# Causal attention with a layer norm and experts: GpSimd's sums of probabilities in four pieces, and the PV matmuls of two key tiles in one run

## What is computed

```python
q = (x @ Wq + bq).reshape(b, s, NQ, D)         # NQ = 16, D = 64
k = (x @ Wk + bk).reshape(b, s, NKV, D)        # NKV = 4
v = (x @ Wv + bv).reshape(b, s, NKV, D)
q = _rotary(q)
k = _rotary(k)
logits = einsum('bqhgd,bkhd->bhgqk', q.reshape(b, s, NKV, g, D), k) / sqrt(D)
logits = where(causal, logits, -1e30)
w = softmax(logits, axis=-1)
out = einsum('bhgqk,bkhd->bqhgd', w, v).reshape(b, s, NQ * D) @ Wo + bo
```

## Time and profile before

| what | value |
|---|---|
| median of 3 runs | 1393.81 us (1393.8 to 1394.24) |
| the profiled execution, its own time | 1390.9 us |
| its span in the profile | 1389.0 us |
| mean granted TensorE clock | 0.972 of 2.4 GHz |
| busy: PE, PEld, DVE, ACT, POOL | 1294.5, 812.5, 919.5, 567.2, 532.4 us |

### The profile page before, as it was taken

How to read it: one execution, slowest core, us unless ns; L and a number is a source line. 1 busy time by engine, 2 the same in 40 slices (tenths; PEclk the granted TensorE clock), 3 DMA queues, 4 the chain that set the end, 5 groups by cost and what they waited for, 6 DMA issues and landing times.

```text
span 1389.0 us, 18379 instructions
## 1 busy us (share of the span) xinstructions
PE 1294.5 (93%) x6732; PEld 812.5 (58%) x6732; DVE 919.5 (66%) x1775; ACT 567.2 (41%) x1178; POOL 532.4 (38%) x503
## 2 busy tenths in 40 slices
PE   3699999988999998999999979999996799999998
PEld 2445555445555554555555545555544688888887
DVE  3767877768687776878777687777747544444443
ACT  1444544544544454454444544453443222232222
POOL 2553346454454554336446345434513211010110
PEclk9699999999999999999999999999997799999999
DMA  5000000000000000000000000000001000000001
GB/s 133 1 0 1 1 1 1 1 1 0 1 0 1 1 1 0 1 1 1 1 0 1 1 1 0 1 1 1 1 1 46 0 24 23 23 23 22 24 1 31
DMA packets 18444, 12.93 MB, mean 9 GB/s; under 512 B 7104, under 2 KB 15680, under 8 KB 18368
## 3 DMA queue, kind: packets, MB, share of 16 engines
q1 hardware_dynamic: 11072, 9.58, 2.3%
q10 hardware_dynamic: 7296, 2.36, 0.7%
HBM read 10.88 MB, written 1.05 MB: 9 GB/s over the span
## 4 chain that ended last, share of the span: by engine, by line
PE 77%; DVE 14%; issue 3%; POOL 3%; ACT 1%; ACTq 1%; DVEq 0%; POOLq 0%
PE PS L1002 17%; PE PS L1050 12%; PE PS L956 10%; PE PS L984 10%; PE PS L1064 8%; PE PS L986 8%; DVE part_max L742 2%; PE PS L1021 2%; PE PS L1012 2%; PE PS L969 2%; DVE k_split L731 2%; DVE full L758 2%; PE PS L933 2%; DVE full L787 2%; PE PS L940 2%
## 5 line engine op out<-in xcount | busy, mean ns | idle before, releaser
L742 DVE TENSOR_REDUCE part_max<-PS 128x1 f32<-128x512 f32 (+2 forms) x576 | 348.8, 620 | 130.0 <-PE PS L956 104.1
L579 ACT ACTIVATE full<-PS 128x512 f32<-128x512 f32 x384 | 224.3, 598 | 230.8 <-PE PS L986 214.6
L956 PE MATMUL PS<-KT,QT 128*128 128x512 f32 (+3 forms) x640 | 263.5, 425 | 9.5 <-ACT QMT L561 5.0
L984 PE MATMUL PS<-QT,KT 128*128 128x512 f32 (+3 forms) x640 | 266.6, 417 | 1.1 <-ACT diag L588 1.1
L986 PE MATMUL PS<-QMT,KT 128*128 128x512 f32 (+3 forms) x640 | 234.4, 366 | 0.0
L448 POOL TENSOR_TENSOR full<-full 128x2048 f32<-128x2048 f32 x32 | 145.7, 4575 | 214.1 <-PE PS L1002 213.6
L956 PEld LDWEIGHTS PS<-KT,QT 128*128 128x128 f32 x640 | 121.7, 193 | 155.8 <-DVE part_max L742 78.8
L1002 PE MATMUL PS<-full,V 128*64 128x512 f32 x768 | 209.5, 624 | 0.0
L588 ACT ACTIVATE diag<-PS 128x512 f32<-128x512 f32 (+3 forms) x256 | 111.3, 438 | 227.9 <-PE PS L989 202.6
L852 DVE TENSOR_TENSOR full<-full,PS 128x512 f32<-128x512 f32 x128 | 88.0, 688 | 145.0 <-ACT full L628 144.9
L984 PEld LDWEIGHTS PS<-QT,KT 128*128 128x128 f32 x640 | 123.2, 193 | 90.8 <-ACT diag L588 32.1
(11 more groups left out here) (109 smaller groups left out, 1636.4 us busy)
## 6 DMA issues: line engine op xcount, KB each, us to landing
full<-in_L_ffn_experts_w_dram SPq DMA_DIRECT2D x24, 256.0 KB, 2.9
out_dram<-XA SPq DMA_DIRECT2D x4, 256.0 KB, 2.3
wqkv<-in_L_attn_Wq_dram ACTq DMA_DIRECT2D x1, 512.0 KB, 4.3
bqkv<-in_L_attn_bq_dram ACTq DMA_DIRECT2D x1, 512.0 KB, 9.4
wo_sb<-in_L_attn_Wo_dram SPq DMA_DIRECT2D x1, 512.0 KB, 8.4
sin_sb<-in_k_sin_dram ACTq DMA_DIRECT2D x1, 512.0 KB, 8.4
full<-in_L_wmod_dram SPq DMA_DIRECT2D x1, 384.0 KB, 9.5
cos_sb<-in_k_cos_dram ACTq DMA_DIRECT2D x1, 256.0 KB, 9.9
```

Of the source, the lines that this page charges most:

```text
L579: nc.scalar.activation(full[:, k % QUADS, r, :], PS[:, bank, :], ACT.Exp).then_inc(probs_ready, 1)
L742: nc.vector.reduce_max(part_max[:, t, b:b + 1], PS[:, bank, 0:width], AX.X).then_inc(ring_dve, 1)
L956: last = nc.tensor.matmul(PS[:, bank, 0:w], QT[:, ch % 2, h, t * P:(t + 1) * P], KT[:, 0, b * BANK:b * BANK + w], start=True, stop=not las ...
L984: nc.tensor.matmul(o, KT[:, 0, kt * P:(kt + 1) * P], QT[:, ch % 2, h, q0:BANK], start=True, stop=False)
```

## The change

Two things. On GpSimd a quad sum with q below the diagonal is four instructions of 128x512, each behind the `pv` of its own key tile, and the last one signals. In the list, the `pv` of key tiles is held back and put out in twos: behind the scores of r = 1 stand the `pv` of (q - 1, 3) and (q, 0), behind the scores of r = 3 those of (q, 1) and (q, 2). A `pv` now weighs nothing, and a marker `gap` with the weight of two `pv` stands behind the scores of r = 0 and 2, so that other steps may be placed there; the marker itself is left out of the final list. The sums of quads move one key tile later. At the end of J = 0 what is held back is put out at once.

```diff
-        return {"pv": 2.1, "qmax": 1.5, "proj": 3.0, "low": 3.0, "qk": 3.5, "poolsum": 0.01, "maxed": 0.25,
+        return {"pv": 0.0, "gap": 4.2, "qmax": 1.5, "proj": 3.0, "low": 3.0, "qk": 3.5, "poolsum": 0.01, "maxed": 0.25,
...
             for r in range(TB):
-                main += [("s", J, q, r, 0), ("s", J, q, r, 1)] + pending
-                if r == 0 and q > 1:
+                main += [("s", J, q, r, 0), ("s", J, q, r, 1)]
+                if r % 2 == 0:
+                    main.append(("gap", J, q, r))
+                else:
+                    main += pending
+                    pending = []
+                if r == 1 and q > 1:
                     if q < CHUNKS - 1:
                         main += [("poolsum", J, m, q - 1) for m in range(2)]
                     else:
                         main += [("quadsum", J, m, part) for m in range(2) for part in range(4)]
-                pending = [("pv", J, q, r)]
+                pending.append(("pv", J, q, r))
+        if J == 0:
+            main += pending
+            pending = []
...
-        return merge([(float(b), x) for b, x in zip(before, main)], [(begin[end], x) for x in pending],
+        return merge([(float(b), x) for b, x in zip(before, main) if x[0] != "gap"], [(begin[end], x) for x in pending],
...
                         if q < ch:
-                            pool.wait_ge(pv_done, n.at["pv", J, q, TB - 1] + 1)
                             a, b = quad_of[J, m, q] % QUADS, quad_of[J, m, q - 1] % QUADS
-                            nc.gpsimd.tensor_tensor(full[:, a], full[:, a], full[:, b], ALU.add)\
-                              .then_inc(pool_added, 1)
+                            for r in range(TB):
+                                pool.wait_ge(pv_done, n.at["pv", J, q, r] + 1)
+                                last = nc.gpsimd.tensor_tensor(full[:, a, r], full[:, a, r], full[:, b, r], ALU.add)
+                            last.then_inc(pool_added, 1)
                             continue
```

## The result

| | before | after |
|---|---|---|
| median (us), lowest to highest | 1393.8, 1389.75 to 1394.24 | 1380.33, 1378.6 to 1381.51 |
| ratio of the runs to those before, 95% interval | | 0.9909, 0.9886 to 0.9931 |
| profiled execution, its span | 1390.9, 1389.0 | 1379.26, 1377.4 |
| mean granted TensorE clock | 0.972 | 0.972 |

The kernel is faster by 13.5 us, 0.97%; the forecast was 50 us. 1380.3 lies above the range. By the profiled executions the gain is 11.6 us.

A forecast was written before the change was run, and what follows sets the result against it. The prediction took TensorE's own stream to bound the kernel through the attention. Merges 46.2 plus pieces 20.8, less 7.5, 2, 1.6 and 6, gave 50 us off 1393.8: 1343.8 us, range 1326 to 1369.

The forecast's parts named there:

- Part 2, the pieces: At the three passages, shorter GpSimd adds free VectorE earlier; TensorE's 5.04 us waits and the slow clock go: 20.8 us.
- Part 1, the price of a merge: In TensorE's stream, each of 152 runs taken out saves 0.35 us: 53.2 us, of which 46.2 reach the end.
- J = 3, of which I had already given away half: In J = 3 VectorE is nearly full, so half the merges' gain counts: 2.8 us off over four groups.
- the other pair steps are less filled, so I take 6: Over the pair steps, `max` steps standing closer together make TensorE wait for VectorE: 6 us lost.
- part 3: What is late next: exponentials 7.5 and 2 us, the last group's end 1.6, closer `max` steps 6, all lost.
- My upper bound was 27: Most that closer `max` steps could cost: TensorE's idle 3% in J = 3, taken over 900 us, 27 us.
- I wrote off four merges at each of three passages: From q = 3 of J = 7 to the end of J = 0 VectorE sets the time: 4.2 us off.
- I forecast 5.7 us for it: Behind the three 5.04 us waits the slow clock goes, 1.9 us each time: 5.7 us gained.
- Late exponentials where nothing stands between two key tiles: TensorE waits 0.5 us for ScalarE at 18 of 160 places, 15 of them counted: 7.5 us lost.
- VectorE becomes the bound: Rival, chance 0.20: VectorE limits the kernel and half of the merges' 46.2 us is kept, 1367 us.
- I wanted to see VectorE's share at 95%: Sign of being wrong: VectorE's share in J = 1 to 6 reaches 95%.
- the 30 that I had named: Sign of being wrong: TensorE's busy time falls by under 30 us.

The follow-up runs named there:

- e1: The kernel before with only GpSimd's adds cut into four pieces, the `pv` left single: 1372.22 us, ratio 0.9873 to the kernel before.
- e4: The changed kernel with the gap's weight halved and given to both places, behind the scores of r = 0 and 2 and behind the `pv` run: 1353.97 us, ratio 0.9745.
- e3: The changed kernel with the second `qmax` of each pair step placed as late as it goes, behind the last scores: 1378.7 us, ratio 0.9916.

## Why the prediction was wrong, step by step

**Part 2, the pieces: right.** 20.8 us were forecast, and e1 gained 17.8, all of it in the three passages (18.3 by the table, 6.1 each for 6.9 forecast). The waits of 5.04 are gone, and so is the slow clock behind them. GpSimd's piece takes 1303 ns for the 1.29 forecast, and its extra time (548.4 busy for 532.4, where I had allowed 0.6 x 32, which is 19 and not 18) is hidden, as said.

**Part 1, the price of a merge: right beside a run, too high over a step.** TensorE in the changed kernel, a run of two:

```profile
655.10 0.40 PE L965 MATMUL PS<-KT,QT 128*128 128x512 f32 x1
655.42 1.94 PE L1011 MATMUL PS<-full,V 128*64 128x512 f32 x8
657.29 0.50 PE L993 MATMUL PS<-QT,KT 128*128 128x512 f32 x1
657.63 0.40 PE L995 MATMUL PS<-QMT,KT 128*128 128x512 f32 x1
```

1.87 us from start to start, with 0.32 ahead and 0.34 behind: what the earlier trace rows gave. So the slow neighbour behind a run is there, beside the drains that the Trainium skill names; by my estimate from that rule alone, 0.20 for a merge, J = 5 and 6 would have given 10.4 us and not 15.2. They gave 0.27 and 0.31 for a merge, though TensorE never stands there (busy for 32.10 of 32.10 and 42.40 of 42.40 us in the third group); at 0.35 it would have been 3 us more, and what takes those was not settled.

**What failed: "the other pair steps are less filled, so I take 6".** That is the last term of part 3, the bunched `max` steps. The table gives its size. By 0.35 a merge J = 2 should have fallen by 5.6 us and didn't; J = 4 should have fallen by 8.4 and rose by 9.1; J = 3, of which I had already given away half, should have fallen by 2.8 and rose by 10.4. Together that is 5.6 + 17.5 + 13.2 = 36.3 us, for 6. My upper bound was 27, and it was no bound: I took TensorE's idle share in the fullest stretch of the *old* order as the worst that a new order could do. I looked at how full VectorE was, and not at what TensorE would still have to do behind its waits for VectorE. J = 3 shows it with nothing left over: in the four groups the second `qmax` comes 1.4 us earlier, and 13.4 us stand behind it instead of 1.6, of which 4 x 1.95 = 7.8 are the work that was moved there and 4.0 the slow clock over it. That was no question of close `max` steps, and the prediction had no term for it. Close `max` steps do cost in J = 4, and in J = 2, by waits for the ring. A `pv` of weight 2.1 between two key tiles did two things: it took 1.21 us, and it held room for other steps. The change moved all of that room to one side.

**Also short: the passages.** I wrote off four merges at each of three passages. Eleven merges a group lie there (2 in J = 1, 9 in J = 7), and between e1 and the change the passages grew by 1.8 us instead of falling by 33 x 0.35 - 4.2 = 7.4: 9 us more. In e4 the merges there bring nothing either (230.0 for 229.7), so I had written off too few of them: VectorE holds more of that stretch than I took. That is argued from the earlier trace rows; no run tested it.

**The clock: given back.** I forecast 5.7 us for it. Before, it fell three times, at the wait of 5.04. In the changed kernel those are gone, and it falls at seven other places, five in J = 3 and 4 and two in J = 0, for 3.4 us each at half speed, 1.7 lost, at most 12 us in all; so the mean is 0.972 again. By stretch, the standstill before one of them, and the stretch behind it:

```profile
394.00:396.20 2.20, 0.10 (x1) 0.10 (x2) 1.99 (x6) 1.13 (x4) 1.06 (x2) 1.00 0.00 0
396.20:399.80 3.60, 3.60 (x18) 2.45 (x18) 1.62 (x3) 1.04 (x3) 3.28 (x5) 0.53 0.00 0
```

and VectorE's and TensorE's timeline at that place:

```profile
395.11 0.68 DVE L751 TENSOR_REDUCE part_max<-PS 128x1 f32<-128x512 f32 x1
395.82 0.17 DVE L757 TENSOR_REDUCE q_max<-part_max 128x4 fp32r<-128x12 f32 x1
396.10 0.33 PE L978 MATMUL PS<-ident,q_max 128*128 128x128 f32 x1 [2.19 <-DVEq L759]
```

TensorE stands for 2.19 us ahead of a `qmax`, whose last maximum VectorE hasn't reduced yet, and the 1.2 GHz level follows. In e1 and e4 the clock doesn't fall between the start and the tail of the attention. Five such falls in J = 3 and 4 would be 8.5 of the 19.5 us lost there, if TensorE set the time throughout. The third group is the better measure, since its clock doesn't fall in these steps: it takes 66.7 us for them instead of 63.2. Four groups like it would lose 14.2 us, so the clock is worth some 5 of the 19.5, and the order the rest.

**The smaller terms held.** Late exponentials where nothing stands between two key tiles: TensorE in the last group, J = 7,

```profile
1006.81 0.39 PE L995 MATMUL PS<-QMT,KT 128*128 128x512 f32 x1
1006.83 1.09 ACT L588 ACTIVATE full<-PS 128x512 f32<-128x512 f32 x2 [1.55 <-PE PS L995]
...
1007.48 0.50 PE L993 MATMUL PS<-QT,KT 128*128 128x512 f32 x1 [0.28 <-ACT full L588]
```

The next scores start 0.67 us behind the last ones, 0.44 more than the usual 0.23; I took 0.5. From the start of that J = 7 to the end of the span e1 took 369.6 us and the change 371.4: 1.8 more, where 8 x 0.5 + 1.6 - 9 x 0.35 = 2.5 were forecast.

Of the rivals, "VectorE becomes the bound" was the nearest in mechanism. It was priced at 23 us, half of the merges' gain, as if VectorE could only cap the gain; the measured loss is 36 to 45 us, all of the gain and more in the steps concerned. And its mark was taken over the wrong stretch: I wanted to see VectorE's share at 95%. In J = 3 of the third group it is at 23.97 of 27.70 us, 87%, lower than the 89% before; from the `proj` to the `qmax`, where it sets the time, it is at 97%. Of my signs of being wrong one came true, if barely: TensorE's busy time fell by 28.8 us, under the 30 that I had named.

## What to carry to other kernels

Price a reorder by what it leaves behind a wait as well as by what it saves. If a second engine sets the moment at which a step can start (here 25.3 us into J = 3, in e4 as in the change), work of the first engine that stands ahead of that step is free and the same work behind it is paid in full. And if other steps go through a small ring of buffers, a longer run wants them on both sides of it, not all on one (here the pairs came out 8 us above e1 with all the room on one side, and 18 us below it with the room split). A long instruction that shuts another engine out may be cut up at little cost (17.8 us gained here); and two parts of one change are measured apart, since a good one can hide that the other does nothing.

## What I had not expected of the hardware

The granted clock fell to the 1.2 GHz level behind a standstill of TensorE of 2.19 us (0.53 over the 3.6 us behind it); in the kernel before I had only seen it at one of 5.04 us. The same program doesn't do so at each of its four groups, which hold the same instructions: J = 3 of the changed kernel took 29.2, 29.3, 27.6 and 28.5 us, while it took 26.1 in each group before. The first, second and fourth have such a fall of the clock, the third has none, though TensorE stands for 2.20 us there. Nor does it take that much: e3 stands for 1.21 us at the same place, and there the clock falls in all four groups. The third group of the change and of e3, from the `qmax` on and over the fall:

```profile
643.10:646.70 3.60, 3.60 (x27) 2.66 (x28) 1.69 (x3) 1.35 (x4) 3.28 (x5) 1.00 0.03 7
```

```profile
644.80:648.20 3.40, 3.40 (x15) 2.34 (x12) 0.40 (x1) 0.94 (x2) 3.16 (x4) 0.50 0.03 7
```

So the length of the standstill by itself doesn't decide; what does, these runs don't show. A kernel with such standstills can take different times in groups that hold the same instructions.
